# Attention output of two head pairs in one group, a new table of side jobs, and a later start of GpSimd's row scaling

## What is computed

```python
q = (layernorm(xn) * g + b) @ Wq;  k, v = split(xn @ Wkv)         # 16 heads of 64
q, k = l2norm(q) * q_scale, l2norm(k) * k_scale                   # two learned null keys and values go in front
sim = q @ k.T * 8 - slope[h] * abs(j - i)                         # 256 x 258, causal
out = softmax(sim) @ v                                            # per head
x = x + concat(out) @ Wout + (silu(xn @ sg.T) * (xn @ su.T)) @ sd.T + routed(xn)
```

## Time and profile before

| | us |
|---|---|
| median of 3 runs | 479.3 (478.34 to 479.67) |
| profiled execution, whole | 479.73 |
| profiled execution, its span | 478.0 |
| PE busy | 421.6 (88%) |
| PE weight loads busy | 305.1 (64%) |
| DVE busy | 366.7 (77%) |
| ACT busy | 357.9 (75%) |
| POOL busy | 294.3 (62%) |

### The profile page before, as it was taken

How to read it: one execution, slowest core, us unless ns; L and a number is a source line. 1 busy time by engine, 2 the same in 40 slices (tenths; PEclk the granted TensorE clock), 3 DMA queues, 4 the chain that set the end, 5 groups by cost and what they waited for, 6 DMA issues and landing times.

```text
span 478.0 us, 10590 instructions
## 1 busy us (share of the span) xinstructions
PE 421.6 (88%) x2793; PEld 305.1 (64%) x2793; DVE 366.7 (77%) x1419; ACT 357.9 (75%) x1097; POOL 294.3 (62%) x444
## 2 busy tenths in 40 slices
PE   3846805999998899999999999999999999999995
PEld 3734503667776676676666776776676677767663
DVE  5699602666652898899799889989988997997884
ACT  3344702666665979988997998899799899989874
POOL 3748779910001589579768848966875894785400
PEclk9969855999999999999999999999999999999998
DMA  8971112222221000000001001000100100010000
GB/s 234 319 247 34 56 49 60 62 73 81 77 73 39 1 25 0 2 24 23 3 1 45 2 1 47 0 2 2 44 2 2 45 2 2 14 32 2 24 23 12
DMA packets 29738, 21.36 MB, mean 45 GB/s; under 512 B 3528, under 2 KB 27376, under 8 KB 29552
## 3 DMA queue, kind: packets, MB, share of 16 engines
q1 hardware_dynamic: 26816, 16.46, 11.7%
q0 software_dynamic: 2048, 4.20, 2.9%
q10 hardware_dynamic: 816, 0.03, 0.1%
HBM read 12.41 MB, written 8.26 MB: 43 GB/s over the span
## 4 chain that ended last, share of the span: by engine, by line
PE 54%; DVE 18%; issue 9%; ACT 8%; POOL 7%; DMA 3%; ACTq 1%; DVEq 0%
POOL slot_x L418 7%; PE bank L1104 7%; PE bank L1095 7%; PE bank L958 6%; PE bank L959 5%; PE bank L960 5%; DVE arena_b L887 4%; PE bank L1053 4%; PE bank L1085 4%; PE bank L1172 4%; PE bank L1118 4%; DVE arena_b L902 3%; DMA arena_b<-slot_x 2%; DVE probT L912 2%; DVE ssq L871 2%
## 5 line engine op out<-in xcount | busy, mean ns | idle before, releaser
L663 ACT ACTIVATE arena_b<-arena_b,nmx 128x130 f32<-128x130 f32 (+1 forms) x256 | 114.9, 458 | 16.3 <-PE bank L1095 8.3
L887 DVE CUSTOM_DVE_ANT_0 arena_b<-bank,bias 128x130 f32<-128x130 f32 (+1 forms) x256 | 81.2, 355 | 29.8 <-PE bank L1104 15.7
L902 DVE TENSOR_SCALAR arena_b<-arena_b,rden 128x130 f32<-128x130 f32 (+1 forms) x256 | 84.9, 375 | 4.5
L431 POOL TENSOR_TENSOR rpow<-ssm,mhalf 128x8 f32<-128x8 f32 x32 | 52.5, 1641 | 45.3 <-DVE ssm L875 45.3
L444 POOL TENSOR_TENSOR arena_b<-arena_b,rnorm 128x512 f32<-128x512 f32 x64 | 66.9, 1045 | 5.1 <-POOL rnorm L434 0.2
L1095 PE MATMUL bank<-ident,arena_b 128*128 128x128 f32 x384 | 67.0, 283 | 2.4 <-DVE arena_b L902 2.3
L1104 PE MATMUL bank<-arena_a 64*128 64x130 f32 (+1 forms) x512 | 59.5, 351 | 0.8 <-ACT arena_a L624 0.8
L1095 PEld LDWEIGHTS bank<-ident,arena_b 128*128 128x128 f32 x384 | 44.1, 141 | 22.0 <-DVE arena_b L902 13.1
L428 POOL TENSOR_TENSOR rnorm<-ssm,mhalf 128x8 f32<-128x8 f32 x32 | 52.7, 1646 | 0.9
L663 ACT ACTIVATION_READ_ACCUMULATOR arena_b<-arena_b,nmx 128x1 f32 x256 | 51.2, 200 | 0.0
L871 DVE TENSOR_REDUCE ssq<-arena_b 128x8 f32<-128x512 f32 x64 | 43.6, 682 | 4.7 <-ACT arena_b L601 3.9
(11 more groups left out here) (196 smaller groups left out, 969.4 us busy)
## 6 DMA issues: line engine op xcount, KB each, us to landing
slot_x<-probT SPq DMA_DIRECT2D x3, 832.0 KB, 8.6
arena_b<-slot_x SPq DMA_DIRECT2D x39, 64.0 KB, 1.9
slot_y<-arena_b SPq DMA_DIRECT2D x39, 64.0 KB, 1.5
arena_a<-in_L_attn_x_dram SPq DMA_DIRECT2D x2, 512.0 KB, 5.3
arena_b<-in_L_ffn_wd_dram SPq DMA_DIRECT2D x1, 1024.0 KB, 9.9
arena_b<-in_L_attn_Wkv_dram SPq DMA_DIRECT2D x1, 1024.0 KB, 8.8
arena_b<-in_L_attn_x_dram SPq DMA_DIRECT2D x8, 128.0 KB, 2.6
out_dram<-arena_b SPq DMA_DIRECT2D x8, 128.0 KB, 2.0
```

The lines of the kernel that those rows point to most:

```text
L663: sc.activation(prob[:, (HEADS * b + h) % RP, c], sim[h % 2][:, c], ACT.Exp, scale=-1.0, bias=nmx[:, h % HEADS, t:t + 1], accum_out=den[:, ...
L887: ve.tensor_tensor_reduce(out=sim[h % 2][:, c], in0=bank[h % 2][:, c], in1=bias[:, c], scale=-SLOPES[h], scalar=3e38, op0=ALU.add, op1=ALU ...
L902: ve.tensor_scalar(pr, pr, rden[:, h % HEADS, t:t + 1], None, ALU.mult).then_inc(g.pn, 1)
```

## The change

**Two pairs together.** The output matmuls (L1085, L1086) of two pairs are issued in one group at every fourth step (heads 4f to 4f+3 at step 4f+7), into a whole bank 4 (`ofour`, 128x512). `probT` has two buffers for each half, `oT` is 512 wide, ACT copies four heads at once at step 4f+8, and the two Wout matmuls stand in one group at step 4f+9. The semaphores `pvd`, `oev` and `oread` count four heads.

**Side jobs.** The table has other steps for them, 14 on side 0 and 10 on side 1 where it was 12 and 12; the jobs themselves are the same 24. On PE they stand at the end of a step, after the Wout matmuls. On DVE a job of side 0 is read out before the row maxima of an odd step, one of side 1 behind them. At step 0 PE waits for two side banks before the first scores. ACT's copy of the finished batch (`yT`) stands behind the exponentials of step 6.

**POOL.** Before it scales a "kq" block at step s, POOL also waits until DVE has normalised head s-1.

```diff
@@ table
-        JOBS = [[(1, "next", "kq", 0, 1, 0), (2, "prev", "pn", 0, 0, 0), (4, "next", "kq", 0, 1, 1), (5, "next", "kq", 0, 0, 0),
-                 (6, "next", "kq", 0, 0, 1), (7, "prev", "yt", 0, 0, 0), (8, "own", "v", 1, 0, 1), (11, "next", "kq", 1, 1, 1),
-                 (12, "next", "kq", 1, 0, 0), (13, "next", "kq", 1, 0, 1), (14, "next", "v", 0, 0, 0), (15, "next", "v", 0, 0, 1)],
-                [(0, "own", "tr", 1, 1, 0), (1, "own", "tr", 1, 1, 1), (2, "own", "tr", 1, 0, 0), (3, "own", "tr", 1, 0, 1),
-                 (4, "own", "v", 1, 0, 0), (5, "own", "sh", 0, 0, 0), (7, "next", "kq", 1, 1, 0), (8, "own", "sh", 1, 0, 0),
-                 (10, "next", "tr", 0, 1, 0), (11, "next", "tr", 0, 1, 1), (12, "next", "tr", 0, 0, 0), (13, "next", "tr", 0, 0, 1)]]
+        JOBS = [[(1, "next", "kq", 0, 1, 0), (2, "prev", "pn", 0, 0, 0), (3, "next", "kq", 0, 1, 1), (4, "own", "tr", 1, 0, 0),
+                 (5, "next", "kq", 0, 0, 0), (6, "next", "kq", 0, 0, 1), (7, "prev", "yt", 0, 0, 0), (8, "own", "v", 1, 0, 1),
+                 (9, "next", "tr", 0, 1, 1), (10, "next", "tr", 0, 0, 0), (11, "next", "kq", 1, 1, 1), (13, "next", "kq", 1, 0, 1),
+                 (14, "next", "tr", 0, 0, 1), (15, "next", "v", 0, 0, 1)],
+                [(0, "own", "tr", 1, 1, 0), (1, "own", "tr", 1, 1, 1), (2, "own", "tr", 1, 0, 1), (3, "own", "sh", 0, 0, 0),
+                 (6, "own", "v", 1, 0, 0), (7, "next", "kq", 1, 1, 0), (8, "own", "sh", 1, 0, 0), (10, "next", "tr", 0, 1, 0),
+                 (11, "next", "kq", 1, 0, 0), (13, "next", "v", 0, 0, 0)]]
@@ POOL
                         norms(job_b, job)
+                        if job[0] == "kq":
+                            pool.wait_ge(g.pn, TB * (HEADS * b + s))
                         scale_by_norm(job_b, job)
@@ ACT
-                    if h is not None and h % 2:
-                        p = h // 2
-                        act.wait_ge(g.pvd, PAIRS * b + p + 1)
-                        if part != "first" or p >= 2:
-                            act.wait_ge(g.oread, PAIRS * b + p - 1)
-                        sc.activation(oT[p % 2][:], opair, ACT.Copy).then_inc(g.oev, 1)
+                    if h is not None and h % 4 == 3:
+                        f = h // 4
+                        act.wait_ge(g.pvd, FOURS * b + f + 1)
+                        if part != "first" or f >= 2:
+                            act.wait_ge(g.oread, FOURS * b + f - 1)
+                        sc.activation(oT[f % 2][:], ofour[:], ACT.Copy).then_inc(g.oev, 1)
@@ DVE
-                    if s % 2 == 1:
-                        row_maxima(part, b, s)
-                    h = head_at(part, s, 3)
-                    for job in behind(part, b, s, 1):
-                        side_out(*job)
+                    done = behind(part, b, s, 1)
+                    for job in done:
+                        if job[2][4] == 0:
+                            side_out(*job)
+                    if s % 2 == 1:
+                        row_maxima(part, b, s)
+                    for job in done:
+                        if job[2][4] == 1:
+                            side_out(*job)
+                    h = head_at(part, s, 3)
                     if h is not None and h % 2 == 0:
                         dve.wait_ge(g.ptps, HEADS * b + h + 1)
-                        if part != "first" or h >= 2:
-                            dve.wait_ge(g.pvd, PAIRS * b + h // 2)
-                        ve.tensor_copy(probT[0][:], bank[2][:, 0:3 * P]).then_inc(g.ptev_d, 1)
+                        if part != "first" or h >= 4:
+                            dve.wait_ge(g.pvd, FOURS * b + h // 4)
+                        ve.tensor_copy(probT[0][h // 2 % 2][:], bank[2][:, 0:3 * P]).then_inc(g.ptev_d, 1)
@@ PE
-                    if h is not None and h % 2:
-                        p = h // 2
-                        if part != "first" or p >= 1:
-                            pe.wait_ge(g.oev, PAIRS * b + p)
-                        for half, evacuated in ((0, g.ptev_d), (1, g.ptev_a)):
-                            pe.wait_ge(evacuated, PAIRS * b + p + 1)
-                            r, hh = slice(half * DH, (half + 1) * DH), 2 * (p % PAIRS) + half
-                            te.matmul(opair[r, 0:SEQ], v[:, 0, hh * DH:(hh + 1) * DH], probT[half][:, 0:SEQ], start=True, stop=False)
-                            ins = te.matmul(opair[r, P:SEQ], v[:, 1, hh * DH:(hh + 1) * DH], probT[half][:, SEQ:3 * P],
-                                            start=False, stop=True)
+                    if h is not None and h % 4 == 3:
+                        f = h // 4
+                        if part != "first" or f >= 1:
+                            pe.wait_ge(g.oev, FOURS * b + f)
+                        for p in (2 * f, 2 * f + 1):
+                            o = p % 2 * SEQ
+                            for half, evacuated in ((0, g.ptev_d), (1, g.ptev_a)):
+                                pe.wait_ge(evacuated, PAIRS * b + p + 1)
+                                r, hh, pT = slice(half * DH, (half + 1) * DH), 2 * (p % PAIRS) + half, probT[half][p % 2]
+                                te.matmul(ofour[r, o:o + SEQ], v[:, 0, hh * DH:(hh + 1) * DH], pT[:, 0:SEQ], start=True, stop=False)
+                                ins = te.matmul(ofour[r, o + P:o + SEQ], v[:, 1, hh * DH:(hh + 1) * DH], pT[:, SEQ:3 * P],
+                                                start=False, stop=True)
                         ins.then_inc(g.pvd, 1)
...
+                        if h == 0 and part != "first":
+                            for i, last in enumerate(LAST_TURNED):
+                                pe.wait_ge(left[i], jobs_until("mid", b - 1, i, last + 1))
```

More of the change, by code:

```diff
@@ L23 @@
 PAIRS = HEADS // 2
+FOURS = HEADS // 4
 K0 = NNULL + P
@@ L119, in build @@
         assert at[0] <= 11008
-        probT = [sb(f"probT{i}", [P, 3 * P]) for i in range(2)]
+        probT = [[sb(f"probT{half}_{i}", [P, 3 * P]) for i in range(2)] for half in range(2)]
         arena_r = sb("arena_r", [P, 2048], F32R)
@@ L135, in build @@
             ring.append([carve_r(SEQ), carve_r(SEQ)])
-        oT = [sb(f"oT{i}", [P, SEQ]) for i in range(2)]
-        opair = bank[4][:, 0:SEQ]
+        oT = [sb(f"oT{i}", [P, 2 * SEQ]) for i in range(2)]
+        ofour = bank[4]
         pnT = sb("pnT", [96, SEQ], F32R)
@@ L266, in behind, with jobs_until @@
             return [(part, b, job) for job in jobs(part, b, s - lag)] if part else []
+        LAST_TURNED = [max(job[0] for job in JOBS[i] if job[1:3] == ("next", "tr")) for i in range(2)]
+        def jobs_until(part, b, i, s):
+            n = count(part, i, s)
+            if part != "ahead":
+                n = n + count("ahead", i)
+                if part != "ready":
+                    n = n + count("ready", i)
+                    if part != "first":
+                        n = n + count("first", i) - count("mid", i)
+                        if part == "drain":
+                            n = n + count("last", i) - count("mid", i)
+                        n = b * count("mid", i) + n
+            return n
         def jobs(part, b, s):
@@ L274, in jobs @@
                         continue
-                    n = count(part, i, s)
-                    if part != "ahead":
-                        n = n + count("ahead", i)
-                        if part != "ready":
-                            n = n + count("ready", i)
-                            if part != "first":
-                                n = n + count("first", i) - count("mid", i)
-                                if part == "drain":
-                                    n = n + count("last", i) - count("mid", i)
-                                n = b * count("mid", i) + n
-                    found.append((*job[2:], i, n))
+                    found.append((*job[2:], i, jobs_until(part, b, i, s)))
             return found
@@ L1106, in entry @@
                         ins.then_inc(g.sps, 2)
-                    for job in todo:
-                        side_job(job, b)
+                    if s == 13 and "own" in whose:
+                        pe.wait_ge(g.sh_h, 2 * b + 2)
+                        for c in range(2):
+                            te.matmul(bank[6][:, 0:SEQ], sd[:, c, :], hs[:, c, :], start=False, stop=False)
                     if s == 5 and "prev" in whose:
@@ L1112, in entry @@
                     h = head_at(part, s, 6)
-                    if h is not None and h % 2:
-                        p = h // 2
-                        if p == 0 and part != "first":
+                    if h is not None and h % 4 == 3:
+                        f = h // 4
+                        if f == 0 and part != "first":
                             pe.wait_ge(g.yev, b)
-                        pe.wait_ge(g.oev, PAIRS * b + p + 1)
-                        te.matmul(bank[6][:, 0:SEQ], wo[:, p % PAIRS, :], oT[p % 2][:], start=p == 0,
```

(16 more changed lines are left out.)

22 lines of the change are left out of this document (11 added, 11 removed).

## The result

The changed kernel takes 471.56 us in the median of 6 runs (469.96 to 474.13), the kernel before 479.56 (478.34 to 481.28) on the same chip. The ratio is 0.9838 with an interval from 0.9806 to 0.9871: 1.6% faster. The span of the profiled execution went from 478.0 to 469.8 us. The forecast was 469.0, with a range from 463 to 478.

A forecast was written before the change was run, and what follows sets the result against it. PE was taken as the bound. Saved switches of 9.6 us and 1.4 us less waiting, against 0.7 us for a longer end, gave -10.3 us: 469.4 from the profiled 479.7, or 469.0 by the median, range 463 to 478.

The forecast's parts named there:

- What bounds the kernel: Whole batch loop: PE is the bound, busy 39.99 of 40.70 us, with ACT and DVE 4 us behind it.
- Switch term: PE's pair outputs: each removed switch into the 64-column form and back saves 0.30 us, 1.20 per batch, 9.6 over the loop.
- the second pair's entry in the open: Output group of two pairs: at worst the second pair's weights load in the open, leaving 0.15 us saved of each 0.30.
- Waiting term: Where PE comes late: waits of 1.4 us per batch become 1.2, 0.2 less in seven batches, 1.4 us.
- The sign that the prediction named against itself: PE over the batch: if its idle time grows, the forecast of less waiting is wrong.
- The worst new place: Step 9 to 10, where DVE is fullest: about 0.8 us of new waiting expected.
- POOL's wait: POOL's scaling against DVE's normalisation: one or two of four collisions go, 0.5 to 1 us of DVE's time, not the bound.
- POOL's cover: Null copies behind POOL's waiting instruction, for which ACT's exponentials wait: 0.5 us of cover before the row maxima end.
- All waits go: Rival, 18%: scaling always starts behind a normalisation, 2.2 us of collisions go, waiting falls to 0.4 per batch; 463.4 us.
- The saved time comes back as waits: Rival, 14%: DVE bounds steps 4 to 10, so waiting grows by what the switches save; 477.6 to 480.0 us.
- POOL is late: Rival, 7%: at step 7 POOL's gathers and null copies start later and hold up ACT; slower, 483.5 us.
- the group isn't one: Rival, 5%: the array serialises the pairs' halves, each output group costs up to 0.65 us more; 490 us.

## Why the prediction was right, and where it was not

**What bounds the kernel.** Right. PE's saved time came through: 1.02 us of switches per batch by the run that restored them, and the batch fell by 1.21. With the scaling cut short PE is idle for 0.01 us in a batch of 38.6, so its own work is what remains.

**Switch term.** The mechanism was right, the size somewhat high: 0.255 us each in place of 0.30, so 8.2 us over eight batches where 9.6 stood. In the rows, 0.09 ahead of the group is still there (324.04 to 324.36, in place of 0.23), and so is 0.05 to 0.06 behind it at steps 3 and 7. Within it 0.12 goes (1.50 for two pairs, in place of twice 0.81), where 0.16 was taken. The bound "the second pair's entry in the open" fell: a group took 1.50, forecast 1.46.

**Waiting term.** The size agrees, the places only in part, so the agreement is partly luck. 1.21 less 1.02 leaves 0.19 us per batch, where the forecast was 0.2; by the price on PE, 1.09, it is 0.12. This is a remainder and not a measured wait. The sign that the prediction named against itself, more idle time of PE, is there in a small way (0.68 to 0.76 us). Steps 3 and 11 have lost their waits as said. The worst new place was looked for at steps 9 to 10, and 0.37 and 0.14 stand there. The largest, 0.48 at step 8, was not named; it is the bank of the "yt" job. The swap of sides moved it to step 9 and won nothing, so both waits go back to DVE.

**POOL's wait.** This step failed. The forecast took it for 0.5 to 1 us of DVE's time off the path, after a look at POOL at steps 6 and 7. It followed the "kq" job that the table moves from step 4 to step 3 on DVE, and not on POOL. There its scaling falls on head 3's normalisation, for which PE is waiting. Without the wait the kernel takes 478.74 us, no gain at all. The total came out only because the change brings the wait with it. What was said of POOL's cover held. In the view of waits for 200 to 440 us, ACT's exponentials never wait for a null copy. After the change they wait for DVE's row maxima alone, and for these more than before; the waits that the view puts down to PE's transposes (8.3 us) are gone, so the sum is a little less (total us, times, longest; first before, then after):

```profile
ACT arena_b L663 <- PE bank L1095: 8.3, 6, 1.4
...
ACT arena_b L663 <- DVE nmx L887: 3.7, 6, 0.7
```

```profile
ACT arena_b L669 <- DVE nmx L898: 10.7, 22, 1.1
```

DVE lost 1.36 us per batch in stretched normalisations, where it was 2.06 before. Heads 2 and 14 are nearly free of it, as one or two of four were forecast to be; head 8 fell from 0.69 to 0.24, head 10 stays at 0.5, and head 15 is new with 0.40. The forecast put all 2.2 us down to the scaling, but head 2 before and head 15 after collide with the splits. Nor is it the wait that frees head 14: with the switches restored and the wait in place it is back (0.8).

**The parts as a sum.** The forecast priced the switches as if they were worth 1.2 us per batch on any table. On the old table, without the wait, the groups give 0.9% more time, and the new table without groups and wait 1.2% more. The group's coverage of waits was counted at steps 3 and 11; that step 13 lost the 0.81 us that covered its "kq" job was not. The cover that an edit takes away has to be looked for at each removed group, as it was for each added one.

**End and first batch.** The end costs 1.15 us (forecast 0.7): behind the longer copy there is a wait of 0.37 us for it as well. Up to head 8 of batch 0 the changed kernel won nothing, though its first normalisation came 1.9 us sooner in the profiled execution. So seven batches paid, and not eight. With 9.3 us of these, less 1.15, the span's 8.2 is accounted for. The forecast's 10.3 was too high by the switch's size (1.4), by one batch's switches (1.0) and at the end (0.45). Against that, the first and the last of the seven won 1.7 and 1.5 us instead of 1.2, some 0.8 more. Why they did stays open, and that it makes good a part of the rest is luck.

**Rivals.** *All waits go* was wrong for this kernel, and its mechanism was borne out: with the scaling cut short the batch is 38.64 us, 2.1 below the kernel before, where this rival had 2.2 (1.2 of switches and 1.0 of waiting). The ratio is 0.971 beside 0.984. That cut also ends each scaling sooner, which the rival did not have. Its rule ("SBUF — State Buffer", Who interferes with whom, in the Trainium skill: the shared ports are locked for a whole instruction) agrees with the row of 1.41 us, in which DVE's second instruction ends 0.16 us behind the scaling. *The saved time comes back as waits* fell for the change as a whole, but it is just what the groups do on the old table (41.11 us per batch), and in large part what they do on the new one without the wait (40.31). *POOL is late* fell, since no exponential waits for a null copy, and *the group isn't one* fell with the 1.50 us of a group.

## What to carry to other kernels

When the engine that sets the time is relieved of something, look at every place that the removed work covered, and not only at the longest wait: a group of 0.8 us taken from one step uncovered a bank wait of 1.1. Where instructions of two engines stretch one another, list after the move each of the one against each of the other (here POOL's scalings and splits against DVE's normalisations), since a job put one step earlier can turn a harmless overlap into one on the path. Run the parts of such a change alone before a part is dropped: here each by itself made the kernel slower, the groups and the table without the wait won nothing, and all three together were 1.6% faster. The wait with one of the other two was not run.

## What the runs showed of the hardware

A GpSimd scaling that begins 0.21 us into a pair of VectorE instructions stretches the pair from 0.55 to 1.41 us, and costs GpSimd itself nothing (1.04 us either way). One that began 0.30 us into it left the pair at 0.55 and took 1.15 itself. GpSimd made to wait 0.50 us for that pair gives VectorE 0.86 back.

Going into the 64-column form of matmul and back costs TensorE 0.255 us, measured in place by restoring four such switches a batch (40.40 against 39.38 us); from start to start on TensorE it is 0.21 to 0.31 by its place, 0.27 in the mean. The Trainium skill ("TensorEngine Tiling (Array Packing)", Key Properties) says that a change of tiling mode drains the engine; the run agrees with it in that each change costs time, 0.255 us for the way in and back, and shows nothing of the drain itself.
